# Layer-0 attention by key tile for four heads, with the exponentials as the stationary operand

## The reference

```python
q = x @ Wq.T                      # (4, 512, 256) -> 16 heads of 16
k, v = jnp.split(x @ Wkv.T, 2, axis=-1)   # one k, one v of 16 features
attn = jnp.einsum('bhqd,bkd->bhqk', q, k) / math.sqrt(HEAD_DIM)
attn = jnp.where(causal[None, None], attn, jnp.float32(-1e9))
attn = jax.nn.softmax(attn, axis=-1)
out = jnp.einsum('bhqk,bkd->bhqd', attn, v)
return out.reshape(bs, seq, D_MODEL) @ Wo.T
```

## Time and profile before

| | us |
|---|---|
| median of three timed runs | 1541.72 (1540.8 to 1543.54) |
| the profiled execution | 1542.26 |
| its span in the profile | 1540.4 |
| TensorE busy | 1388.5 (90%) |
| VectorE busy | 1055.3 (69%) |
| ScalarE busy | 734.4 (48%) |
| GpSimd busy | 545.8 (35%) |

### The profile page before, as it was taken

The page is one execution under the profiler, slowest core; times in us unless marked ns, Lnnn a source line. Parts: engine busy times, 40 slices in busy tenths (PEclk is TensorE's granted clock), DMA queues, the critical chain, the costliest instruction groups (busy, mean ns, idle before and its releaser), DMA issues.

```text
span 1540.4 us, 26928 instructions
## 1 busy us (share of the span) xinstructions
PE 1388.5 (90%) x8028; PEld 976.7 (63%) x8028; DVE 1055.3 (69%) x3153; ACT 734.4 (48%) x1737; POOL 545.8 (35%) x497
## 2 busy tenths in 40 slices
PE   5988999899898469999999999999999899996998
PEld 3543343334333357778768777877877787885887
DVE  5765457666665686876787687778766866766674
ACT  2334544444444136545654654565456556543332
POOL 0000000000000048898888898888880310000000
PEclk8898999999999579999999999999999999998999
DMA  4120000010102110120011021011200200000000
GB/s 159 41 82 11 22 11 22 21 38 22 38 0 65 45 60 11 37 82 27 19 37 37 9 82 35 7 34 34 89 8 27 74 20 18 27 0 0 14 14 28
DMA packets 28832, 54.21 MB, mean 35 GB/s; under 512 B 4640, under 2 KB 20848, under 8 KB 28256
## 3 DMA queue, kind: packets, MB, share of 16 engines
q1 hardware_dynamic: 25520, 42.80, 8.5%
q0 software_dynamic: 2096, 6.51, 1.4%
q10 hardware_dynamic: 1152, 4.19, 0.7%
HBM read 41.87 MB, written 11.63 MB: 35 GB/s over the span
## 4 chain that ended last, share of the span: by engine, by line
PE 59%; DVE 27%; issue 10%; ACT 3%; DVEq 1%; DMA 0%; ACTq 0%; SPq 0%
PE bank L1184 10%; PE bank L1275 10%; PE bank L1253 7%; PE bank L255 4%; DVE qkst L951 4%; PE bank L257 4%; PE bank L256 4%; DVE qk L970 4%; PE bank L1264 4%; PE bank L1160 3%; PE bank L1048 3%; PE bank L1171 2%; PE bank L1243 2%; PE bank L324 1%; DVE negmax L983 1%
## 5 line engine op out<-in xcount | busy, mean ns | idle before, releaser
L501 POOL TENSOR_SCALAR gtmp<-gidx,lut 128x344 f32<-128x344 int32 (+2 forms) x210 | 302.4, 1440 | 21.3
L881 DVE TENSOR_REDUCE negmax<-bank 128x1 f32<-128x128 f32 (+3 forms) x256 | 123.7, 488 | 124.3 <-PE bank L1173 118.9
L628 ACT ACTIVATE probs<-bank 128x512 f32<-128x512 f32 (+3 forms) x256 | 111.5, 438 | 192.0 <-PE bank L1162 180.3
L1184 PE MATMUL bank<-probs,vS 128*32 128x512 f32 (+3 forms) x512 | 187.8, 449 | 12.8 <-ACT oRaw L646 8.0
L494 POOL DMA_DIRECT2D gidx<-in_idx_gate x4 | 2.2, 560 | 554.7 <-DMA h_saved<-wft 554.7
L504 POOL TENSOR_TENSOR gacc<-gacc,gtmp 128x344 f32<-128x344 f32 (+2 forms) x210 | 184.0, 876 | 17.5
L1253 PE MATMUL bank<-kT,qT 128*128 128x128 f32 (+3 forms) x512 | 179.7, 441 | 8.3 <-ACT probs L694 8.3
L1275 PE MATMUL bank<-pT,v 128*128 128x128 f32 x1280 | 155.4, 277 | 12.2 <-ACT pT L687 12.2
L1275 PEld LDWEIGHTS bank<-pT,v 128*128 128x128 f32 x1280 | 148.0, 192 | 15.9 <-DVE oL L993 15.9
L983 DVE TENSOR_REDUCE negmax<-bank 128x1 f32<-128x128 f32 (+3 forms) x256 | 123.5, 485 | 49.7 <-PE bank L1254 48.3
L694 ACT ACTIVATE probs<-bank,negmax 128x128 f32<-128x128 f32 (+3 forms) x256 | 135.6, 530 | 45.5 <-DVE negmax L983 42.3
(11 more groups left out here) (192 smaller groups left out, 2906.3 us busy)
## 6 DMA issues: line engine op xcount, KB each, us to landing
hH<-h_saved SPq DMA_DIRECT2D x16, 512.0 KB, 3.9
hL<-h_saved SPq DMA_DIRECT2D x16, 512.0 KB, 4.7
qst<-q_parts SPq DMA_DIRECT2D x96, 64.0 KB, 2.3
wg<-in_wqkv SPq DMA_DIRECT2D x4, 1536.0 KB, 8.1
wo<-in_wo SPq DMA_DIRECT2D x4, 512.0 KB, 9.1
out<-x SPq DMA_DIRECT2D x8, 256.0 KB, 2.1
x<-in_x SPq DMA_DIRECT2D x1, 1536.0 KB, 9.8
wmod<-in_wmod SPq DMA_DIRECT2D x1, 1536.0 KB, 11.6
```

Source lines behind the costliest of these rows:

```text
L501: link(pool.tensor_scalar(tmp if j else acc, part, float(j), lut1[0:rows, j:j + 1], ALU.is_equal, ALU.mult))
L1184: pe.matmul(bank[5][rows, k * P:], vS[:, k, :], probs[:, i % 4, 0:SEQ - k * P], start=(k == 0), stop=(k == QT - 1)).then_inc(pv0, 1)
```

## The change

The unit of work becomes a key or query tile for several heads. `UNITS` lists, for j = 0 to 3, tiles of width 512, 384, 256 and 128 with 1, 1, 2 and 4 heads, so that a unit fills at most 512 columns. A group of four heads has 11 units (`GU`), a batch 44 slots (`SLOTS0`). Each unit has one mask matmul, one reduction and one exponential.

The exponentials of a group lie in four tiles `pT0[k]`, by key tile, with four heads in each. The value product (new line 1210) takes 128 x 128 pieces of them as the stationary operand and 17 columns of `vS` as the moving one. When the last unit of key tile k is exponentiated (`ENDS`), TensorE does all four heads for that tile: 16, 12, 8 and 4 matmuls. The output has queries on partitions at once, in one bank for the group; `oRaw`, its copy and its transposes go.

The maxima are split in two bf16 parts instead of three. TensorE turns 32 columns at once, ScalarE makes one copy to `nmt`, and SyncE writes rows 96 and 97 of `qst` by two DMAs (`load_negmax`), which now stand between the reloads of q. `TURN` is 17, `VALUE` 19 and `AFTER` 21. `after0` does the same work in 44 slots, with several norm steps in one (`NORM_SLOTS`). The loop over the two middle batches is written out.

```diff
-TURN = 29
+UNITS = tuple((j, h, n) for j, n in enumerate((1, 1, 2, 4)) for h in range(0, HG, n))
+GU = len(UNITS)
+SLOTS0 = NG * GU
+ENDS = {max(u for u in range(GU) if UNITS[u][0] == j): j for j in range(QT)}
+NMP = 2
+ROWS0 = SHIFT + NMP
+TURN = 17
...
+            def load_negmax(b, g):
+
+                sp.wait_ge(nm_copied, b * NG + g + 1)
+                for j in range(NMP):
+                    sp.dma_start(qst[SHIFT + j:SHIFT + j + 1, g * HG * SEQ:(g + 1) * HG * SEQ].rearrange(
+                        "p (i q) -> p i q", q=P), nmt[j * ITEMS:(j + 1) * ITEMS, :]).then_inc(nm_ready, 16)
...
                     i, batch = at_step(n, VALUE, b, scores, values)
-                    if i is not None:
-                        h, k = i // QT, i % QT
-                        rows = slice(h % HG * VW, (h % HG + 1) * VW)
-                        if i == 0:
-                            pe.wait_ge(v_moved, batch + 1)
-                        if i % ITEMS == 0:
-                            pe.wait_ge(o_copied, batch * NG + i // ITEMS)
-                        pe.wait_ge(exp0, batch * ITEMS0 + i + 1)
-                        pe.matmul(bank[5][rows, k * P:], vS[:, k, :], probs[:, i % 4, 0:SEQ - k * P],
-                                  start=(k == 0), stop=(k == QT - 1)).then_inc(pv0, 1)
...
+                    if i is not None and i % GU in ENDS:
+                        g, k = i // GU, ENDS[i % GU]
+                        if k == 0:
+                            pe.wait_ge(oev0, batch * NG + g)
+                        pe.wait_ge(exp0, batch * SLOTS0 + i + 1)
+                        for h in range(HG):
+                            for t in range(k, QT):
+                                at = (t * HG + h) * VW
+                                last = pe.matmul(bank[5][:, at:at + HD0 + 1], pT0[k][:, h, (t - k) * P:(t - k + 1) * P],
+                                                 vS[:, batch * QT + k, 0:HD0 + 1], start=(k == t == h == 0), stop=(k == t == QT - 1 and h == HG - 1))
+                        last.then_inc(pv0, 1)
```

## The result

The changed kernel takes 1648.75 us (median of four timed runs, 1644.12 to 1655.2); the kernel before, timed beside it, 1542.45 us. The ratio is 1.069 with a 95% interval of 1.065 to 1.073. The profiled execution took 1651.3 us.

The account below looks back on a forecast made before the run. TensorE was taken as the bound; its 279 us of stage work at a low-clock share of 0.7 lasts 429 us, 65 more than 364.0. With the start's 6 less: 1542.3 + 65 - 6 = 1601 us, range 1565 to 1657.

Parts of the forecast that it names:

- The value product, 8.9 us a group: First layer's attention: 80 records per four-head group at 0.1115 us, paced by weight loads, 8.9 us against 10.5 before.
- Scores and edge, 6.4 + 1.0 us: Per group: scores with four hand-overs instead of 16, 6.4 us against 7.9; group edge charged 1.0 us, between 0 and 2.
- full-clock group of 16.4: One four-head group at full clock: 8.9 + 6.4 + 1.0 = 16.4 us, 4.0 less than before.
- VectorE, 12 us: After-attention pieces between reductions, which two score banks can't cover: 12 us charged over the stage at full clock, between 0 and 25.
- The start, 6 us less: Scores-only stretch before the values: 17 slots instead of 29, 14.5 us against 20.9, so 6 us less.
- The maxima's DMAs and the unrolled loop, nothing: Two DMAs carrying the maxima land in time, and writing out the middle-batch loop costs nothing: both counted as zero.
- The clock, a low share of 0.7: Value stage: short matmuls drop TensorE to 1.2 GHz for share s of 0.7 (ends 0.6, 0.85): 429 us, 65 more.
- my own 279 us of work: TensorE's own full-clock work in the stage, without 16 us of edge waits; it lasts 279/(1 - s/2), s the low share.
- Rival 1: The clock holds in the value stage: 1479 us (1465 to 1495), faster than before; chance 0.15.
- rival 2: The clock is low only part of the time, s = 0.2 to 0.55: 1500 to 1557 us; chance 0.20.
- rival 3: Clock low throughout, far above 1657 us, or the maxima come late, adding up to 32 us; chance 0.07.
- rival 4: VectorE bounds the middle batches, 63 us of work in 79.5, only at full clock; priced in Rival 1, no separate chance.

Follow-up runs that it names:

- 128-column kernel: The changed kernel with 128 instead of 17 columns moving in each value matmul, so the value product computes something else: 1507.56 us, ratio 0.977.
- 32-column one: The changed kernel with 32 instead of 17 columns of v moving in each value matmul: 1639.21 us, ratio 1.059.
- twin without the swap: The changed kernel with the value product of before (v stationary, exponentials moving, four heads in a row), oRaw and its transposes: 1471.8 us, ratio 0.949.
- spread order: The changed kernel with 3 or 4 value matmuls of 32 columns per slot: 1680.18 us; with 12 useless bf16 matmuls ahead of each group: 1580.28 us.

## Why the prediction held, point by point

**The bound.** TensorE bounds the stage, and its clock decides. Right: the long waits of the other engines in the stage are for TensorE, and 106 of the 109 us are in the stage, where its clock is 0.57.

**The value product, 8.9 us a group.** Right by the first burst: 0.113 us a record. In the 128-column kernel the four bursts of a group take 3.71 + 2.73 + 1.84 + 0.94 = 9.2 us. At the low level a record takes 0.215 us, close to the 0.21 foreseen. The Trainium skill (TensorE: Matmul & The Clock Gate, "Back-to-back issue gap") gives about 81 ns for a pair of load and matmul at 128 columns. No row of the value product shows it: with 128 columns behind each load a record takes 0.116 us (3.71/32).

**Scores and edge, 6.4 + 1.0 us, and the full-clock group of 16.4.** The 128-column kernel, which kept its clock, runs a group in 16.49 us (160.06 to 176.55), a stage of 317.5 us where I had 307, and 1508 us in all where I had 1479. The part of the sum that did not depend on the clock was good to 2%, as far as a kernel that streams more columns can stand for it.

**VectorE, 12 us.** Plausible: in the 128-column kernel TensorE waits 10.0 us for the reductions of line 905 within the stage. In the changed kernel it is 2.6 us: at the low clock VectorE waits for TensorE (247.2 us at line 905), so the charge is absorbed.

**The start, 6 us less.** Wrong. The first score product of the changed kernel:

```profile
112.68 0.39 PE L1197 MATMUL bank<-kst,qst 96*128 96x512 bf16 x1 [0.75 <-ACT mod L567]
```

From there to 125.6 us scores stand alone: 12.9 us (14.5 predicted), but I let the stage begin there. The first value product comes at the end of a whole key tile, three slots after `VALUE`, so 22 slots pass, the last ones with two score products each: 5.1 us more. That is the step that failed. The scores also begin later in this execution, at 112.68 us instead of 109.3, which is not the change's doing: with the same code up to there they begin at 108.22 us in the 128-column kernel and at 108.94 us in the 32-column one. Together the stage starts 0.6 us later than before.

**The maxima's DMAs and the unrolled loop, nothing.** Right for the DMAs: TensorE never waits long for them. The unrolled loop left no mark, but was not tried by itself.

**The clock, a low share of 0.7.** This is the mis-sized term. A mean of 0.57 is a share of (1 - 0.57)/0.5 = 0.86, just beyond the end of my range (0.85). Of the 50 us between 1601 and the profiled 1651.3 us, 41 are the stage (106 us longer, 65 in my sum), 6.6 the start and 2.5 the rest. I had let the dense spells win the clock back once or twice in every group of some 26 us; it stayed low for 115 us on end. I took the low value because it was nearest to rows where the clock survived, when I had argued myself that bursts at 1.2 GHz last twice as long.

That the time still fell in the range is in part luck. With the share that came and my own 279 us of work, the stage would last 279/0.57 = 489 us, and the kernel 1542.3 + 125 - 6 = 1661 us, above the range's 1657. The stage took 470 us, as if TensorE's work were 268 us (470 x 0.57). One reason shows in the rows: a short record takes 0.215/0.113 = 1.90 times as long at the low level, where my formula has 2. The rest of the difference is not traced.

**The rivals.** Rival 1 (the clock holds) did not come. The Trainium skill (TensorE: Matmul & The Clock Gate, "Why this matters for your kernels") ties such drops to idle gaps between bursts. Here the clock was low without a gap, at 0.50 for 30.00 us in which TensorE was busy for 30.00, so gaps are not the only way down; what gaps alone do, no run here tests. Rivals 2, 3 and 4 did not come either; the maxima were never late. One figure of rival 2 doesn't follow from the sum: by the formula of the forecast its lower end, s = 0.2, gives 279/0.9 = 310 us and a time of 1482 us, not 1500. Only the edge waits and VectorE's charge, which the formula leaves out, could lift it.

**What neither forecast nor rivals held.** I priced the swap against 10.5 us of value product, the price that the old order pays. The new units make another order possible, four heads next to each other, in which the old operands cost 2.7 us. So the swap is 9.2 - 2.7 = 6.5 us more of TensorE's work in a group even at full clock, 104 us in 16 groups. The changed kernel and its twin without the swap differ by 177 us (1648.75 and 1471.8). The 128-column kernel, which has the swap and keeps its clock, parts them: it takes 1507.56 us. So some 36 us are the whole price of the swap at full clock, and the other 141 us are the clock's. The twin's stage idles for 57 us and runs at 0.88, which is probably what hides the rest of the 104 us.

## What to carry to other kernels

Before you swap operands to get a better output layout, count what streams behind each weight load: with 128 x 128 fp32 loads a record took 0.113 us for 17 columns and 0.116 us for 128, so having few of them saved next to nothing. Here they cost the clock as well, a factor of nearly two on what TensorE does nearby. Put matmuls that use different 32-partition strips of the output directly behind each other: here four then cost about what one does, and score products between them take that away. A busy TensorE is no proof of a fast one; read the granted clock of the stretch before anything else.

## What the runs showed of the hardware

- The granted clock stood at 1.2 GHz for 30.00 us in which TensorE was busy for 30.00 us, and later for 115 us on end (busy for 112.24). With 128 moving columns behind the same loads, it was 0.99 in the stage; with 17, 0.57; with 32 in the same burst order, 0.60.
- The same spread order of matmuls runs at either level: it stayed at 0.50 for 136 us, and with a dense spell ahead of each group at 0.98 for 76 us, 1.00 in the 14 us between two spells.
- fp32 matmuls on four 32-partition strips of one bank, issued next to each other, take 0.79 us for 384 columns, against 0.76 us for one. With bf16 score products between them each pays for itself.
- A record of a 128 x 128 fp32 load and its matmul takes 0.113 us at full clock and 0.215 us at the low level with 17 columns, and 0.116 us at full clock with 128.
- Not settled: why the kernels without the swap run at 0.88 in the stage when their heads are adjacent and at 0.97 when they are apart. The first has more idle time (56.7 against 26.2 us) and value matmuls that run side by side, and no run here separates the two.
